# A four-layer graph network on one core: the factors that weigh the gathered rows move from SBUF to PSUM

## What is computed

```python
x = _layernorm(x + _L0_gnn_ref(...))   # attention with 4 heads: out = segment_sum(alpha * xh[row], col)
x = _layernorm(x + _L1_gnn_ref(...))   # segment_sum(edge_weight[:, None] * x[src], dst), then a small MLP
x = _layernorm(x + _L2_gnn_ref(...))   # segment_sum(proj[src, edge_type] * attn_mean[:, None], dst), layer norm, relu
x = _layernorm(x + _L3_gnn_ref(...))   # segment_sum(h[src] * alpha[:, None], dst), softmax over a node's edges
```

## Time and profile before

| | us |
|---|---|
| median of three runs | 8133.76 |
| the profiled execution's own time | 8117.26 |
| its span, first to last instruction | 8115.4 |
| DVE busy | 3856.3 (48%) |
| POOL busy | 5361.6 (66%) |
| ACT busy | 679.1 (8%) |
| PE busy | 894.4 (11%) |

### The profile page before, as it was taken

One profiled execution on the slowest core, in us unless ns is written; L12 is line 12 of the kernel. 1 busy time (PEld: TensorE's weight loads), 2 busy tenths in 40 slices (PEclk: granted clock), 3 DMA queues, 4 the chain that ended last, 5 costly groups with the idle time before them and its releaser, 6 DMA issues. The chain is left out here.

```text
span 8115.4 us, 26187 instructions
## 1 busy us (share of the span) xinstructions
PE 894.4 (11%) x3516; PEld 558.6 (7%) x3516; DVE 3856.3 (48%) x8781; ACT 679.1 (8%) x1577; POOL 5361.6 (66%) x5178
## 2 busy tenths in 40 slices
PE   7500000000000000000025555000000001000000
PEld 5500000000000000000013222000000001000000
DVE  8994454313354343333335665668333334345256
ACT  1021111000000010000013333000000003000002
POOL 0067777767767747777745666666777756767764
PEclk9996555555555555555557877555555555555555
DMA  2081000213333323322225766332332221333332
GB/s 49 1 304 28 2 2 2 57 22 96 87 101 102 91 89 96 95 89 88 93 73 178 250 244 234 101 106 73 96 96 90 92 88 53 82 91 112 83 100 64
DMA packets 275316, 770.98 MB, mean 95 GB/s; under 512 B 122571, under 2 KB 132993, under 8 KB 237129
## 3 DMA queue, kind: packets, MB, share of 16 engines
q0 software_dynamic: 166224, 282.97, 14.7%
q1 hardware_dynamic: 90708, 375.35, 12.8%
q10 hardware_dynamic: 18210, 111.02, 3.6%
HBM read 357.59 MB, written 411.37 MB: 95 GB/s over the span
## 5 line engine op out<-in xcount | busy, mean ns | idle before, releaser
L2172 POOL DMA_INDIRECT l2s_krow<-table_k,l2s_idx x784 | 770.1, 982 | 417.3 <-issue 253.5
L753 POOL DMA_INDIRECT l2z_rows<-proj,l2z_idx x784 | 852.3, 1087 | 254.0 <-issue 238.8
L753 POOL DMA_INDIRECT l3z_rows<-table,l3z_idx x784 | 802.5, 1024 | 304.4 <-issue 237.1
L753 POOL DMA_INDIRECT l1z_rows<-table,l1z_idx x784 | 829.0, 1057 | 263.2 <-issue 239.3
L753 POOL DMA_INDIRECT l0z_rows<-table,l0z_idx x784 | 811.2, 1035 | 285.7 <-issue 239.6
L1707 POOL DMA_INDIRECT first_sj<-scores,first_atdst x784 | 807.1, 1029 | 256.4 <-issue 256.4
L729 DVE SCALAR_TENSOR_TENSOR l1z_acc<-l1z_acc,g_dokeep,l1z_msg 128x128 f32<-128x128 f32 x784 | 278.0, 355 | 569.6 <-DVE l1z_acc L729 379.2
L729 DVE SCALAR_TENSOR_TENSOR l2z_acc<-l2z_acc,g_dokeep,l2z_msg 128x128 f32<-128x128 f32 x784 | 277.8, 354 | 499.1 <-DVE l2z_acc L729 316.0
L729 DVE SCALAR_TENSOR_TENSOR l0z_acc<-l0z_acc,g_dokeep,l0z_msg 128x128 f32<-128x128 f32 x784 | 277.7, 354 | 396.5 <-DVE l0z_acc L729 283.3
L2109 DVE SCALAR_TENSOR_TENSOR l2s_qrow<-l2s_qrow,g_dokeep,l2s_zrow 128x82 f32<-128x82 f32 x1568 | 367.3, 300 | 192.0 <-DVE l2s_qrow L2109 123.1
L2127 PE MATMUL l2s_bank<-l2o_wr,l2s_fed 128*128 128x512 f32 x800 | 415.7, 679 | 301.7 <-ACT l2s_fed L2151 162.0
(11 more groups left out here) (543 smaller groups left out, 3544.4 us busy)
## 6 DMA issues: line engine op xcount, KB each, us to landing
proj<-l2s_proj ACTq DMA_DIRECT2D x100, 1024.0 KB
spread_q<-prep_zero SPq DMA_DIRECT2D x98, 656.0 KB
l2s_zrow<-spread_q SPq DMA_DIRECT2D x98, 656.0 KB
prefix<-l3z_acc SPq DMA_DIRECT2D x48, 1040.0 KB
prefix<-l0z_acc SPq DMA_DIRECT2D x48, 1024.0 KB
prefix<-l1z_acc SPq DMA_DIRECT2D x48, 1024.0 KB
prefix<-l2z_acc SPq DMA_DIRECT2D x48, 1024.0 KB
first_sj<-scores,first_atdst POOLq DMA_INDIRECT x784
```

What stands on the lines that cost most here:

```text
L753: nc.gpsimd.indirect_dma_start(out=rows[:, k % RING, u, :], out_offset=None, in_=table, in_offset=bass.IndirectOffsetOnAxis(ap=idx[:, lo + ...
L2172: nc.gpsimd.indirect_dma_start(out=krow[:, h, u, :], out_offset=None, in_=g.table_k, in_offset=bass.IndirectOffsetOnAxis(ap=idx[:, h, u:u ...
```

## The change

The weighing reads its factors from PSUM. Three classes are touched:

- `Weighed` (l1z, l2z) gets a PSUM tile `factors` of 128 x 784 and copies the factors into it with one DVE instruction in the first batch; all weighings read it.
- `Attended0` (l0z): the last of the small instructions that make the shares writes to a PSUM tile `share` (two halves, used in turn) instead of back to `a`; the weighing reads it.
- `Online3` (l3z): the exponential of the 2 x 16 differences, one ACT instruction, becomes two of 16: the edges' shares go to one of two PSUM tiles, the decays of the old sum to SBUF. DVE waits for both. The weighing and the scan L868 read the share from PSUM.

The accumulations (L729), the gathers, the stores and the rest of the program stay as they are.

```diff
@@ class Weighed
+        self.factors, self.known = s.ps("factors", [P, NC]), s.sem("known")
...
     def weigh(self, eng, chain, k, lo, hi, before):
         n = hi - lo
-        self.v.tensor_tensor(self.msg[:, 0:n], self.rows[:, k % RING, 0:n, 0:D], bc_last(self.weight[:, lo:hi], D), ALU.mult).then_inc(self.weighed, 1)
+        if k == 0:
+            self.v.tensor_copy(self.factors[:], self.weight).then_inc(self.known, 1)
+            eng.wait_ge(self.known, 1)
+        self.v.tensor_tensor(self.msg[:, 0:n], self.rows[:, k % RING, 0:n, 0:D], bc_last(self.factors[:, lo:hi], D), ALU.mult).then_inc(self.weighed, 1)
         eng.wait_ge(self.weighed, k + 1)
@@ class Attended0
+        self.share = s.ps("share", [P, 2, WIDTH, HEADS])
...
-        chain(v.tensor_tensor(a, b, rows[:, :, D + 8:D + 12], ALU.mult))
+        share = self.share[:, k % 2, 0:n]
+        chain(v.tensor_tensor(share, b, rows[:, :, D + 8:D + 12], ALU.mult))
         v.tensor_tensor(self.msg[:, 0:n].rearrange("p u (w c) -> p (u w) c", w=HEADS),
                         rows[:, :, 0:D].rearrange("p u (w c) -> p u w c", w=HEADS),
-                        bc_last3(a, D // HEADS), ALU.mult).then_inc(self.weighed, 1)
+                        bc_last3(share, D // HEADS), ALU.mult).then_inc(self.weighed, 1)
@@ class Online3
-        self.x = s.sb("xx", [P, 2, 2, WIDTH])
+        self.x, self.share = s.sb("xx", [P, 2, WIDTH]), [s.ps(f"share{h}", [P, WIDTH]) for h in range(2)]
...
-        eng.wait_ge(self.es, k + 1)
-        v.tensor_tensor(self.msg[:, 0:n], rows[:, :, 0:D], bc_last(x[:, 1], D), ALU.mult).then_inc(self.weighed, 1)
-        chain.add(v.tensor_tensor_scan(out[:, :, D + 1], x[:, 0], x[:, 1], before[:, D + 1:D + 2], ALU.mult, ALU.add))
+        eng.wait_ge(self.es, 2 * (k + 1))
+        v.tensor_tensor(self.msg[:, 0:n], rows[:, :, 0:D], bc_last(share, D), ALU.mult).then_inc(self.weighed, 1)
+        chain.add(v.tensor_tensor_scan(out[:, :, D + 1], x, share, before[:, D + 1:D + 2], ALU.mult, ALU.add))
...
-        self.nc.scalar.activation(self.x[:, k % 2, :, 0:n], self.d[:, k % 2, :, 0:n], ACT.Exp).then_inc(self.es, 1)
+        self.nc.scalar.activation(self.share[k % 2][:, 0:n], self.d[:, k % 2, 1, 0:n], ACT.Exp).then_inc(self.es, 1)
+        self.nc.scalar.activation(self.x[:, k % 2, 0:n], self.d[:, k % 2, 0, 0:n], ACT.Exp).then_inc(self.es, 1)
```

More of the change, by code:

```diff
@@ L803, in __call__ @@
         self.b = s.sb("b", [P, 2, WIDTH, HEADS])
-        return super().__call__(nc, s, us, es, weighed, order, rows, msg, acc)
+        self.share = s.ps("share", [P, 2, WIDTH, HEADS])
+        self.rows, self.msg, self.v, self.order, self.weighed = rows, msg, nc.vector, order, weighed
+        return self
     def weigh(self, eng, chain, k, lo, hi, before):
@@ L852, in factor @@
     def factor(self, k, lo, u):
-        return self.x[:, k % 2, 0, u:u + 1]
+        return self.x[:, k % 2, u:u + 1]
     def weigh(self, eng, chain, k, lo, hi, before):
         n, h = hi - lo, k % 2
-        v, e, old, d, x = self.v, self.e[:, 0:n], self.old[:, 0:n], self.d[:, h, :, 0:n], self.x[:, h, :, 0:n]
+        v, e, old, d, x, share = self.v, self.e[:, 0:n], self.old[:, 0:n], self.d[:, h, :, 0:n], self.x[:, h, 0:n], self.share[h][:, 0:n]
         rows, out, gap, most = self.rows[:, k % RING, 0:n], self.acc[:, k % ACCS, 0:n], self.gap[:, lo:hi], self.most[:, 1 + lo:1 + hi]
@@ L2194, in layers1_to_3 @@
                 tab2 = Tables2(nc, q, g, a, wr)
-                sum_messages(nc, "l1z", g, O.dst, g.table1, g.prefix, D, Weighed(g.weight), tab2)
+                sum_messages(nc, "l1z", g, O.dst, g.table1, g.prefix, D, Weighed(g.weight[:]), tab2)
                 tail1(nc, g, O, tab2, xT)
@@ L2201, in layers1_to_3 @@
                 attention = Attention(nc, q, g, base[:], qv[:], attn[:])
-                sum_messages(nc, "l2z", g, O.dst, g.proj, g.prefix, D, Weighed(attn), Beside(attention, tab3))
+                sum_messages(nc, "l2z", g, O.dst, g.proj, g.prefix, D, Weighed(attn[:]), Beside(attention, tab3))
         with Space(nc, "l3h") as s:
```

## The result

The changed kernel takes 8146.10 us (median of 20 runs, 8127.44 to 8173.99) against 8108.84 us (20 runs, 8036.30 to 8138.81): a ratio of 1.005, 95% interval 1.0034 to 1.0067. The forecast was 7950 us.

What follows compares the result with a forecast made beforehand. POOL's 784 gathers at 1.25 us (980 us) were taken as most of each pass, with DVE spaced and lagging. 174 us arriving, less 2 for copies and 2 for the exponential, gave 170 off 8117.26: 7950 us, range 7860 to 8060.

Steps and rivals of the forecast that it cites:

- point 1: POOL's gathers beside weighings: holds vanish, 1.2 us for each of 50 batches, 60 us per pass, 240 us in all.
- point 2: Ends of the four passes: of the 240 us saved on POOL, 40, 43, 43 and 48 arrive, 174 us.
- point 3: Weighing on DVE: reading factors from PSUM costs 0; ends 0 and a doubled 2.29 us.
- points 4, 5: Two copies in l1z and l2z, at most 1 us each; l3z's second exponential, 229 ns per batch, charged 2 us.
- B: Accumulations, also with two SBUF inputs, fall into step with gathers, slowing POOL to 1.40 us: 8040 us, chance 0.17.
- C: DVE's spacing goes with the holds or comes later: 7685 us if all gone, about 7820 if half; chance 0.15.
- D: DVE does not shake off its spacing, l3z recovers later, 13 us per further spaced batch: slower, 8270 us, chance 0.05.
- E: Gathers beside weighings stay held, the cause being other than the second SBUF input: nothing freed, 8120 us, chance 0.06.

Runs made afterwards that it cites:

- e1: The change with its factors back in SBUF in all four passes, the second exponential kept, against the kernel before: 1.0014.
- d4: The change with 15 of the 16 accumulations of each batch left out (output not the network's): passes of 1075, 1072, 1087 and 1076 us.
- s2: The change with one accumulation and one scan per batch for 16 accumulations, but weighing factors in SBUF: 1.0305 of before on the 7487 us chip.
- s1: The change with one accumulation and one scan per batch in place of 16 accumulations, weighing factors in PSUM: 0.9732 of before on the 7487 us chip.
- The scan with its factors in PSUM: The change with each batch's 16 accumulations made one accumulation and one TENSOR_TENSOR_SCAN, weighing factors in PSUM: 0.9892 and 0.9732 of before on two chips.
- f1: The change with a GpSimd pause of four scratch writes per batch, from the eleventh batch on: 0.9904 of before.
- e5: The kernel before the change with a GpSimd pause of two scratch writes in each batch of gathers: 1.0288 of before on the 7487 us chip.

## Why the prediction was wrong

1. *Holds removed* (point 1): right in mechanism, somewhat too large in size. POOL's busy time fell by 42 and 47 us in l0z and l3z, where 60 were taken, and on the chip of 7487 us the change with a ring of 3 is 187 us faster. The change with its own ring of 6 met no such chip, so the 187 us are shown for a ring of 3 alone. In l1z and l2z the holds went and the 1.09 us gathers came in their place, 1.40 us to the next.
2. *What reaches the end* (point 2): **the step that failed.** I let 174 of the 240 us arrive, since POOL's own 1.25 us per gather seemed to pace the gathers and VectorE's spacing seemed a state that would stay as it was. Nothing arrived. After some 190 gathers they go at 1.40 us whatever POOL could do, so the last gather of each pass starts where it did (1 us later, 0 and 1 earlier, 5 later); in l0z and l3z POOL spent what it had gained in 40 and 24 us more of waits at the full ring. POOL, faster at first, is ahead sooner and more batches are spaced: 4 more in l0z, 3 in l1z, 9 in l2z, 5 in l3z. The time lost is VectorE's lag behind the last gather, which went from 62, 53, 47 and 8 us to 50, 55, 55 and 46. Nearly all of it is l3z, where the last spaced run now lies near the end; l0z, with more spaced batches too, is 11 us shorter. Instead of -174 the passes gave +39.
3. *Weighing from PSUM* (point 3): 2288 ns against 2294, cost 0, as taken. The fixed cost that the Trainium skill ("VectorE: DVE Perf Modes", section on the TRN2 errata) gives PSUM sources isn't seen at this size.
4. *Copies and second exponential* (points 4, 5): small, as taken. e1 gives 1.0014 with an interval that holds 1. Its l3z is 13 us longer, with fewer spaced batches but a lag of 47 us in place of 8, since its last spaced run lies at the end; whether the second exponential has a part in that is open.

Of the rivals, B foresaw the gathers at 1.09 us but put them down to the accumulations' two SBUF inputs; d4 has the 1.40 us with one accumulation per batch. C had the spacing thin out, and it grew. D named the direction and the place (l3z recovers later) and got a chance of 0.05; at its price, 13 us for each spaced batch more, the 5 of l3z would be 65 us where 43 were lost. That there is a pace of gathers below POOL's own, the "in step" 1.09 + 0.30 of the earlier trace rows, stood in the rows and I read it as a collision, not as a limit. E was wrong: the holds go with a PSUM operand, also against the sentence of the Trainium skill ("SBUF — State Buffer", section Who interferes with whom) that the prediction gives; s2 and its twin s1 show it once more (3.44 against 0.94 us).

What holds the gathers to 1.40 us, and why on four of the five chips of the experiments and not on the fifth, stays open; no run here looks inside it. Open too is why the accumulations are spaced beside it and shorter chains are not.

## The better version

The scan with its factors in PSUM is faster than the kernel before on either kind of chip: 0.9892 where before takes 8092 us and 0.9732 where it takes 7487; there the change with a ring of 3 is nearly as good (0.9752). Where gathers are limited, f1 (0.9904, on another chip) comes level with it by three lines of pausing, but probably costs time where they are not: e5, before with a pause, takes 1.0288 there.

## What to carry to other kernels

Before removing a wait of a producer, compare its own pace with the slowest steady pace in the trace: if the producer with its waits (here 1.33 us per gather) is already faster than that (1.40), the wait costs nothing and its removal brings nothing. The start of the last gather, before and after, tells at once whether a saving on the producer arrives. Regular gaps of one length on several engines suggest one shared pace, so test it with a kernel whose suspected chain is short. And ask for more than one chip: what costs 0.5% to 1.0% wherever the change ran (three times) is worth 2.5%, with a ring of 3, on a chip without the limit.

## What was not expected of the hardware

- Gathers have a sustained pace of 1.40 us each on four chips of five, with 128 or with 64 rows, after about 190 gathers at 1.25 us; on one chip 784 went at 1.25. The rows land as fast on either kind.
- While POOL is ahead and VectorE works through its 16 accumulations, a dependent instruction on VectorE starts 1.05 us after the one before it has ended, and one on GpSimd 0.9 us, once 4.30 us, while the gathered data land in time. With shorter chains on VectorE none is late.
- A TENSOR_TENSOR_SCAN with one operand in PSUM lets gathers pass; at 4.42 us for 2048 columns it costs about twice the weighing.
